# Two-layer graph convolution on one core: who issues the row-by-row tiles, the edges and the broadcasts of the inverse counts

## The chip, the core and the metric

The kernel runs on one core of one Trainium2 chip. The metric is the time of one execution on the device in microseconds (us). PE is TensorE, DVE is VectorE, ACT is ScalarE, POOL is GpSimd and SP is SyncE, which only issues transfers here.

## What is computed

Two layers of an edge-conditioned graph convolution over 6250 nodes with 128 features and 100000 edges with 64 features, edges sorted by destination, then a layer norm of the sum with the input:

```python
def _cgconv(x, src, dst, edge_attr, Wf, bf, Ws, bs, gamma, beta, rmean, rvar):
    z = jnp.concatenate([x[dst], x[src], edge_attr], axis=-1)
    msg = jax.nn.sigmoid(z @ Wf + bf) * jax.nn.softplus(z @ Ws + bs)
    summed = jax.ops.segment_sum(msg, dst, num_segments=n)
    cnt = jax.ops.segment_sum(jnp.ones((dst.shape[0],), x.dtype), dst, num_segments=n)
    out = summed / jnp.maximum(cnt, 1.0)[:, None]
    out = (out - rmean) * jax.lax.rsqrt(rvar + BN_EPS) * gamma + beta
    return out + x
x = _layernorm(x + two_layers(x), axis=-1)
```

## The kernel before

**Tiling.** Edges are padded to 49 groups of 2048. A group has 4 slots (`j`), a slot has 4 tiles of 128 edges, seven groups are a body (`k`), and a layer is 7 bodies: 196 slots, numbered on through the layer in what follows. The first body is written out, the other six are a loop (`Fori`), whose end jumps back five times a layer. Transfers are issued by SP, and gathers by POOL.

**Before the loop.** PE multiplies all node columns with the source half of the weights, ACT copies the result out, and SP stores it as rows of `s_dram` (the source term of z @ W for every node, 256 numbers, 1 KB). The first seven slots of a layer don't wait for that and gather plain node rows.

**A slot.** POOL gathers the source rows of its four tiles into one of 7 places of `pre` (`gather`, L409), by the source numbers in `ends`; it waits until softplus has freed the place seven slots back. DVE overwrites the destination half of the edge columns `lhs` with a transposed one-hot (`hot_transposed`, L791). PE multiplies `lhs`, that is one-hot and edge features, with `rhs` (`product`, L527) into one of two banks `pre_ps`. DVE adds this to the gathered rows in `pre` (`sums`, L815). ACT then has five activations for the slot: two exponentials (L632, L633), two logarithms (L637, L639) and the gate's exponential (L643). DVE makes softplus (L819) and the message (L826), PE sums the messages over the destinations with a one-hot (L801) in a window of 64 nodes (`window_sum`, L548), and DVE adds the window to `sums` (L851). ACT also copies the destination term into `rhs` two slots ahead (L626) and window columns (L649), and reads the windows' bases once a group (`next_bases`, L656).

DVE's order in the step of slot m is fixed: L791 for m, the one-hot L801 for m, L851 for m-4, L815 for m-1, L819 and L826 for m-2. ACT's order is L626, L649, L632, L633, L637, L639, L643.

**SP in the loop (`one`, L353).** For each half group (two slots) SP waits for a product (L362), loads the edge columns of two slots into one of two places of `lhs` (L267, 512 KB), at the first half also the next group's `ends` and bases (L222, L263), and then does a part of the work for a single tile: tile 3 of slot 27 of each body (`SINGLE`) isn't gathered by POOL. SP fetches its block number and its 128 source numbers into `sp_src`, reads 12 of them at a time into registers (L331), and issues one transfer of 1 KB for each row (L335) into `single`; at the end of the body one transfer places them in `pre` (L342).

**Waits.** An instruction carries a wait for a semaphore, and the waits that don't fit are instructions of their own. `done(eng, sems, g, j, lag)` waits for the slot `lag` back.

**Between the layers (`invert_counts`, L235).** In its tail layer 1 writes the counts of edges per node to memory (L241), reads them back spread over 128 partitions (L243), DVE inverts them (L843, L845), SP writes them (L245) and broadcasts the inverses to all partitions in five pieces (L248). SP waits for all of it, and then the layer ends for all engines. Layer 2 begins on DVE with five pairs L760 and L763, which make the nodes of layer 2 out of `sums` and the inverses.

Of the kernel before, what the change touches and what calls it, by code (L numbers as in the profile page):

```python
# [1 line left out]

# [5 lines left out]
ALU = mybir.AluOpType  # L8
# [7 lines left out]
P = 128  # L16
# [27 lines left out]
SINGLE = (BODY - 1, SLOTS - 1, TILES - 1)  # L44
SINGLE_ROWS = 12
# [14 lines left out]
GENERAL_AT = GROUPS + 1  # L60
TABLE_ROWS = GENERAL_AT + GENERAL_GROUPS + 2

# [11 lines left out]
def graph_layer(nc, t, d, layer):  # L74
    first = layer == 1
    with nc.cleanup_on_exit(), ExitStack() as ctx:
# [5 lines left out]
        sp_tab = sb("sp_tab", [1, ROW + 1], I32)  # L82
# [9 lines left out]
        sp_blk = sb("sp_blk", [1, 1], I32)  # L92
        sp_src = sb("sp_src", [1, P], I32)
        single = sb("single", [P, F2], F32)
# [40 lines left out]
        list_in, singles_in, single_in = sem("list_in"), sem("singles_in"), sem("single_in")  # L135
        passed = sem("waits_passed")
        if first:
            dsts_in, ends_of_pairs_in, bn_in = sem("dsts_in"), sem("ends_of_pairs_in"), sem("bn_in")
            iotas, cleared, gen_ready, filled = sem("iotas"), sem("cleared"), sem("gen_ready"), sem("filled")
            table_out = sem("table_out")  # L140
            flagged, plan, fast_ready = sem("flagged"), sem("plan_chain"), sem("fast_ready")
            split, bias_split = sem("bias_parts"), sem("bias_split")
# [10 lines left out]
            fast_rows = sb("fast_rows", [1, GROUPS + 2, ROW], I32)  # L153
# [3 lines left out]
        else:  # L157
            rows_turned, rows_staged, rows_out = sem("rows_turned"), sem("rows_staged"), sem("rows_out")
            scaled = sem("scaled")
# [60 lines left out]
        def _(sp):  # L220
# [4 lines left out]
            if first:  # L225
                load_ends(0, 0)
                sp.dma_start(t["w_node"][:, 0, F2:2 * F2], d["w_node"][0, :, F2:2 * F2]).then_inc(w_src_in, 16)
                for c in range(CHUNKS):
                    sp.dma_start(t["x_t"][:, CUTS[c]:CUTS[c + 1]], d["xT"][:, CUTS[c]:CUTS[c + 1]]
                                 ).then_inc(x_in[c], 16)  # L230
                    if c == 2:
                        sp.dma_start(t["w_node"][:, 0, 0:F2], d["w_node"][0, :, 0:F2]).then_inc(w_in, 16)
                sp.dma_start(t["w_node"][:, 1, :], d["w_node"][1]).then_inc(w_in, 16)

            def invert_counts():  # L235
                cnt_row = t["cnt_dram"].rearrange("(a n) -> a n", a=1)
                cnt_cols = t["cnt_dram"].rearrange("(p c) -> p c", p=P)
                inv_row = t["inv_dram"].rearrange("(a n) -> a n", a=1)
# [14 lines left out]
            def entries(at, n, top):  # L253
                return nc.values_load_multi_w_load_instructions(
                    sp_tab[:, at:at + n], engines=[ENG.SP], min_val=0, max_val=top,
                    skip_runtime_bounds_check_because="every entry of the table is clamped")[1]

            def load_table(row):
                sp.dma_start(sp_tab[:], table[bass.ds(row, ROW + 1)].rearrange("(a c) -> a c", a=1)
                             ).then_inc(sp_tab_in, 16)  # L260
# [8 lines left out]
            def read_plan():  # L269
# [6 lines left out]
                load_table(at)  # L276
# [31 lines left out]
            def load_list(b, half):  # L308
                if half == 0:
                    sp.dma_start(sp_blk[:], table[bass.ds(at + group_no(b, SINGLE[0]) * ROW, 1)].rearrange(  # L310
                        "(a c) -> a c", a=1)).then_inc(list_in, 16)
                    return
                sp.wait_ge(list_in, b * 32 + 16)
                sp.sem_inc(passed, 1)
                blk = sp.value_load(sp_blk[:, 0:1], min_val=0, max_val=GROUPS - 1)
                tile = 2 * (SINGLE[1] * TILES + SINGLE[2])
                sp.dma_start(sp_src[:], d["ends"][bass.ds(blk * P, P), tile:tile + 1].rearrange("p c -> c p")
                             ).then_inc(list_in, 16)

            def load_singles(b, part):  # L320
                if part == 0:
                    sp.wait_ge(list_in, b * 32 + 32)
                    sp.sem_inc(passed, 1)
                    if isinstance(b, int):
                        for r in range(len(s_stage)):
                            sp.wait_ge(s_out[r], stores_of(r))
                    else:
                        sp.wait_ge(single_in, b * 16)
                        sp.sem_inc(passed, 1)
                rows = range(part * SINGLE_ROWS, min((part + 1) * SINGLE_ROWS, P))  # L330
                at_row = nc.values_load_multi_w_load_instructions(  # L331
                    sp_src[:, rows[0]:rows[-1] + 1], engines=[ENG.SP], min_val=0, max_val=NPAD - 1,
                    skip_runtime_bounds_check_because="sources are rows of the table")[1]
                for p, r in zip(rows, at_row):
                    sp.dma_start(single[p:p + 1, :], s_dram[bass.ds(r, 1), :]).then_inc(singles_in, 16)  # L335

            def place_singles(b, g):
                sp.wait_ge(singles_in, b * (16 * P) + 16 * P)
                sp.sem_inc(passed, 1)
                done(sp, s_soft, g, SINGLE[1], RING)  # L340
                sp.sem_inc(passed, 1)
                sp.dma_start(pre[:, slot(*SINGLE[0:2]), SINGLE[2], :], single[:]  # L342
                             ).then_inc(single_in, 16)

            def singles(b, half):
                if half < 2:
                    load_list(b, half)
                elif (half - 2) * SINGLE_ROWS < P:
                    load_singles(b, half - 2)
                if half == 2 * BODY - 1:  # L350
                    place_singles(b, group_no(b, SINGLE[0]))

            def one(b, k):  # L353
                g = group_no(b, k)
                sp.wait_ge(sp_tab_in, g * 16 + 16)
                sp.sem_inc(passed, 1)
                blk, = entries(0, 1, GROUPS - 1)
                blk_next, = entries(1 + GPAIRS, 1, GROUPS - 1)
                load_table(at + (g + 1) * ROW)
                for j in range(0, SLOTS, 2):  # L360
                    done(sp, s_prod, g, j, 3)
                    sp.sem_inc(passed, 1)  # L362
                    if not (isinstance(g, int) and g == 0):
                        load_edges(j, blk * GROUP + j * STEP)
# [7 lines left out]
                    singles(b, 2 * k + j // 2)  # L372
# [5 lines left out]
            sp.wait_ge(sp_tab_in, groups * 16 + 16)  # L378
# [5 lines left out]
        def _(pool):  # L384
            if first:
                nc.gpsimd.memset(fast_rows[:], 0).then_inc(cleared, 1)
                nc.gpsimd.iota(gen_rows[:, :, 0], [[1, GROUPS]], base=0, channel_multiplier=0).then_inc(gen_ready, 1)
                nc.gpsimd.iota(gen_rows[:, :, 1:ROW], [[0, GROUPS], [0, GPAIRS]], base=0, channel_multiplier=WIN
                               ).then_inc(gen_ready, 1)
                pool.wait_ge(cleared, 1)  # L390
                nc.gpsimd.iota(fast_rows[:, 0:GROUPS, 0], [[1, GROUPS]], base=0, channel_multiplier=0
                               ).then_inc(cleared, 1)
# [10 lines left out]
                pool.wait_ge(gen_ready, 2)  # L403
# [10 lines left out]
            if first:  # L414
# [3 lines left out]
                pool.dma_start(table_rows[0:GROUPS + 1, :].rearrange("(a r) c -> a r c", a=1),  # L418
                               fast_rows[:, 0:GROUPS + 1, :]).then_inc(table_out, 16)
                pool.dma_start(table_rows[TABLE_ROWS - 2:TABLE_ROWS, :].rearrange("(a r) c -> a r c", a=1),  # L420
                               fast_rows[:, GROUPS:GROUPS + 2, :]).then_inc(table_out, 16)
# [718 lines left out]
```

## Time and profile before

| | |
|---|---|
| time, median of 3 runs | 2084.61 us (2081.55 to 2085.21) |
| the profiled execution | 2084.45 us, its span 2082.7 us |
| PE, matmuls | 1531.5 us, 74% of the span |
| DVE | 1741.5 us, 84% |
| ACT | 1618.2 us, 78% |
| POOL | 1485.8 us, 71% |
| mean granted clock of TensorE | 0.942 |
| POOL, L409 | 1498 gathers, 1416.8 us |
| DMA engines, mean | 163 GB/s |

Busy times leave out register, branch, semaphore and transfer-issuing instructions, and an engine's share is a mean over prologue, layers and tail. `SPq` and `ACTq` in the rows below are those engines' sequencers, which issue transfers and run register instructions.

### The profile page before, as it was taken

To read this page: it belongs to the slowest core of one execution; us is meant where nothing else is said; L and a number is where in the kernel's file an instruction comes from. 1 tells how busy PE (TensorE), PEld (TensorE's weight loads), DVE (VectorE), ACT (ScalarE), POOL (GpSimd) and SP (SyncE) were. 2 spreads that over 40 slices of the span, in tenths; PEclk is the share of its full clock that TensorE was granted. 3 is DMA by queue.
4 is the path that set the end of the run, shared out by engine and by line. 5 is a ranking of instruction groups with operands and counts; after the bars stand their busy time and mean duration, and the time that the engine had idled before them with its cause. 6 is when DMAs were issued, how large, how long until landed. Compare 5 with 4: busy or idle time off the path is not lost. (4 is left out here: it accounts for less than half of the span.)

```text
span 2082.7 us, 41091 instructions
## 1 busy us (share of the span) xinstructions
PE 1531.5 (74%) x8321; PEld 1258.9 (60%) x8321; DVE 1741.5 (84%) x3576; ACT 1618.2 (78%) x3692; POOL 1485.8 (71%) x1579
## 2 busy tenths in 40 slices
PE   6877777767777777677587777777677777776773
PEld 5766666656566666566476566565556566665662
DVE  3799998979889888798648999798888887988887
ACT  3799887878778777787467888787787787977884
POOL 7577777777777777777257777777777777777770
PEclk8999999999999999999799999999999998999995
DMA  8455555555555555555375555555555555555552
GB/s 282 121 161 171 170 160 159 169 160 160 160 164 163 163 162 162 160 158 162 130 244 160 170 169 169 157 164 167 158 162 160 162 164 159 166 164 158 161 148 62
DMA packets 168890, 339.48 MB, mean 163 GB/s; under 512 B 62702, under 2 KB 93030, under 8 KB 168643
## 3 DMA queue, kind: packets, MB, share of 16 engines
q0 software_dynamic: 73824, 200.29, 32.4%
q1 hardware_dynamic: 93298, 135.27, 21.7%
q10 hardware_dynamic: 1522, 1.72, 0.3%
q14 instruction: 223, 1.83, 0.3%
q8 instruction: 23, 0.38, 0.1%
HBM read 315.49 MB, written 19.81 MB: 161 GB/s over the span
## 5 line engine op out<-in xcount | busy, mean ns | idle before, releaser
L409 POOL DMA_INDIRECT pre<-s_rows,ends x1498 | 1416.8, 946 | 477.9 <-issue 444.9
L527 PE MATMUL pre_ps<-rhs,lhs 128*128 128x256 f32 x3136 | 825.3, 406 | 459.3 <-DVE lhs L791 458.5
L527 PEld LDWEIGHTS pre_ps<-rhs,lhs 128*128 128x128 f32 x3136 | 588.2, 197 | 675.5 <-DVE lhs L791 425.5
L815 DVE TENSOR_TENSOR pre<-pre_ps,pre 128x1024 f32<-128x1024 f32 x378 | 460.6, 1218 | 53.9 <-DMA pre<-s_rows,ends 52.7
L632 ACT ACTIVATE logs<-pre 128x512 f32<-128x512 f32 x392 | 246.9, 630 | 304.5 <-DVE pre L815 268.6
L791 DVE SCALAR_TENSOR_TENSOR lhs<-lhs,base_f,sum_ps 64x256 f32<-64x256 int32 x784 | 374.1, 477 | 107.0 <-issue 52.8
L548 PEld LDWEIGHTS sum_ps<-hot,msg 128*128 128x128 f32 x3136 | 431.4, 200 | 44.7 <-issue 14.0
L548 PE MATMUL sum_ps<-hot,msg 128*128 128x64 f32 x3136 | 411.7, 276 | 19.7 <-DVE sums L851 19.7
L626 ACT COPY rhs<-dst_ps 64x256 f32<-64x256 f32 x792 | 290.0, 366 | 54.0 <-issue 27.3
L826 DVE TENSOR_TENSOR msg<-soft_ps,logs 128x512 f32<-128x512 f32 x392 | 271.1, 691 | 13.3
L819 DVE SCALAR_TENSOR_TENSOR soft_ps<-soft_ps,pre 128x512 f32<-128x512 f32 x392 | 270.4, 690 | 1.1 <-ACT soft_ps L639 1.1
L512 PE MATMUL dst_ps<-w_node,x_cols 128*128 128x256 f32 x792 | 263.1, 415 | 6.2 <-ACT rhs L626 4.2
L637 ACT ACTIVATE logs<-logs 128x512 f32<-128x512 f32 x392 | 246.7, 629 | 12.5
L851 DVE TENSOR_TENSOR sums<-sums,sum_ps 128x64 f32 (+1 forms) x784 | 195.1, 249 | 57.1 <-PE sum_ps L548 4.7
L633 ACT ACTIVATE logs<-pre 128x512 f32<-128x512 f32 x392 | 240.4, 613 | 0.0
L643 ACT ACTIVATE logs<-logs 128x512 f32<-128x512 f32 x392 | 240.2, 613 | 0.0
L639 ACT ACTIVATE soft_ps<-logs 128x512 f32<-128x512 f32 x392 | 228.3, 582 | 0.0
L801 DVE TENSOR_TENSOR hot<-sum_ps,rel 128x256 f32<-128x256 f32 x392 | 166.3, 424 | 12.3
L649 ACT COPY x_cols<-x_t 128x64 f32 x784 | 153.2, 242 | 9.5
L512 PEld LDWEIGHTS dst_ps<-w_node,x_cols 128*128 128x128 f32 x792 | 122.8, 196 | 9.7 <-issue 9.6
L514 PE MATMUL dst_ps<-bias_b,ones_b 128*128 128x256 bf16 x396 | 108.7, 275 | 0.0
L409 POOL DMA_INDIRECT pre<-x_rows,ends x56 | 53.4, 954 | 25.7 <-issue 16.2
(95 smaller groups left out, 575.3 us busy)
## 6 DMA issues: line engine op xcount, KB each, us to landing
lhs<-dge_and_destination_cols SPq DMA_DIRECT2D x196, 512.0 KB
single<-s_rows SPq DMA_DIRECT2D x1792, 1.0 KB
pre<-s_rows,ends POOLq DMA_INDIRECT x1498, 2.8
s_rows<-logs SPq DMA_DIRECT2D x8, 512.0 KB
s_rows<-x_t SPq DMA_DIRECT2D x7, 512.0 KB, 9.4
s_rows<-msg SPq DMA_DIRECT2D x6, 512.0 KB, 10.0
x_rows<-pre SPq DMA_DIRECT2D x12, 256.0 KB
out<-y_out SPq DMA_DIRECT2D x12, 256.0 KB, 2.3
```

What stands on the lines that cost most here:

```text
L409: nc.gpsimd.indirect_dma_start(pre[:, slot(k, j), i, 0:width], None, rows, bass.IndirectOffsetOnAxis(ap=ends[:, k, j * TILES + i, 0:1], ax ...
L512: nc.tensor.matmul(dst_ps[:], x_cols[:, j].rearrange("p q w -> p (q w)"), t["w_node"][:, layer - 1, 0:F2], start=True, stop=False)
L527: ins = nc.tensor.matmul(pre_ps[:, j % 2, i, :], lhs[:, j // 2, edges], rhs[:, j, i // 2, :], start=True, stop=not plain(b, k, j))
L548: ins = nc.tensor.matmul(sum_ps[:, q, 0, 0:WIN], msg[:, j, 2 * q + i, :], hot[:, j, 2 * q + i, :], start=i == 0, stop=i == 1)
L626: ins = nc.scalar.copy(rhs[hot_rows[q], j, q, :], dst_ps[hot_rows[q], :])
L632: nc.scalar.activation(logs[:, j % 2, :, 0:F], pre[:, at, :, 0:F], ACT.Exp, scale=-1.0)
L633: nc.scalar.activation(logs[:, j % 2, :, F:F2], pre[:, at, :, F:F2], ACT.Exp).then_inc(s_expo[j], 1)
L637: nc.scalar.activation(logs[:, j % 2, :, 0:F], logs[:, j % 2, :, 0:F], ACT.Ln, bias=1.0).then_inc(s_log_f[j], 1)
L791: ins = nc.vector.scalar_tensor_tensor(lhs[hot_rows[q], j // 2, at], lhs[hot_rows[q], j // 2, at].bitcast(I32), base_f[hot_rows[q], k, PAI ...
L815: nc.vector.tensor_tensor(rows, pre_ps[:, j % 2], rows, ALU.add).then_inc(s_pre[j], 1)
L819: nc.vector.scalar_tensor_tensor(soft_ps[:, j % 2], soft_ps[:, j % 2], SOFT_TOP, pre[:, at, :, F:F2], ALU.min, ALU.max).then_inc(s_soft[j], 1)
L826: nc.vector.tensor_tensor(msg[:, j], soft_ps[:, j % 2], logs[:, j % 2, :, 0:F], ALU.mult).then_inc(s_msg[j], 1)
```

## The change

1. POOL gathers 109 tiles a body and not 111. Three tiles a body are now loaded row by row. SP loads tile 3 of slots 15 and 26 (`SP_TILES`), which the host leaves with 104 edges each by spreading the padding over them (`SHORT_ROWS`), ACT loads tile 3 of slot 27 with 128 rows (`ACT_TILE`). `SP_PARTS` says which rows SP issues in which half group.
2. ACT reads 12 row numbers into registers in every second slot from slot 2 of a body on (`row_numbers`) and issues six rows a slot: one behind each of L632, L633, L637 and L639, two behind L643 (`load_row`).
3. All loads of edge columns move from SP to ACT, which issues them behind the rows that follow L643 of every odd slot (`load_edges`). The last one of a layer loads columns that nobody reads, and SP waits for it before the layer ends, ahead of `invert_counts`.
4. Block numbers are read once a body, 12 (SP) and 8 (ACT) at a time, and not once a group.
5. SP places ACT's tile at the start of the next body (`place_act`), and its own two in half groups 7 and 13.
6. Layer 1 ends once the inverses are in memory. SP issues the five broadcasts as its first work of layer 2, and DVE waits for each piece (`inv_in`).
7. Small ones: `single` is cleared once a layer (so that the 24 rows nobody loads are finite), semaphores of the prologue are merged, and the table has ten more rows at either end.

```diff
+SP_TILES = ((3, 3), (6, 2))
+ACT_TILE = (6, 3)
+SHORT_ROWS = 104
+SP_PARTS = ((0, 0, 12), (0, 12, 32), (0, 32, 44), (0, 44, 60), (0, 60, 72), (0, 72, 92), (0, 92, 104),
+            (1, 0, 16), (1, 16, 28), (1, 28, 48), (1, 48, 60), (1, 60, 76), (1, 76, 88), (1, 88, 104))
+LIST_AT, PLACE_AT = (BODY + 4, 3), (BODY, 2 * BODY - 1)
+ACT_FROM, ACT_ROWS = 2, 6
+            else:
+                inv_row = t["inv_dram"].rearrange("(a n) -> a n", a=1)
+                for c in range(CHUNKS):
+                    sp.dma_start(t["sums"][:, 1, CUTS[c]:CUTS[c + 1]],
+                                 inv_row[:, CUTS[c]:CUTS[c + 1]].to_broadcast([P, CUTS[c + 1] - CUTS[c]])
+                                 ).then_inc(inv_in[c], 16)
...
                 sp.wait_ge(cnt_moved, 48)
-                for c in range(CHUNKS):
-                    sp.dma_start(t["sums"][:, 1, CUTS[c]:CUTS[c + 1]],
-                                 inv_row[:, CUTS[c]:CUTS[c + 1]].to_broadcast([P, CUTS[c + 1] - CUTS[c]])
-                                 ).then_inc(cnt_moved, 16)
-                sp.wait_ge(cnt_moved, 48 + 16 * CHUNKS)
...
+            def load_rows(i, lo, hi):
+                at_row = nc.values_load_multi_w_load_instructions(
+                    sp_src[:, i, lo:hi], engines=[ENG.SP], min_val=0, max_val=NPAD - 1,
+                    skip_runtime_bounds_check_because="sources are rows of the table")[1]
+                for p, r in zip(range(lo, hi), at_row):
+                    sp.dma_start(single[p:p + 1, i, :], s_dram[bass.ds(r, 1), :]).then_inc(singles_in, 16)
...
                 for j in range(0, SLOTS, 2):
                     done(sp, s_prod, g, j, 3)
                     sp.sem_inc(passed, 1)
-                    if not (isinstance(g, int) and g == 0):
-                        load_edges(j, blk * GROUP + j * STEP)
...
+            place_act(bodies)
+            for j in range(0, SLOTS, 2):
+                sp.wait_ge(edge_in[j // 2], groups * 16 + 16)
             sp.sem_inc(passed, 1)
             if first:
                 invert_counts()
...
-                    gather(s_dram, F2, k, j, TILES - ((k, j) == SINGLE[0:2]))
+                    gather(s_dram, F2, k, j, TILES - ((k, j) in SINGLES))
...
+            def load_edges(g, j, blk):
+                done(act, s_prod, g, j, 0)
+                act.sem_inc(passed, 1)
+                act.dma_start(lhs[:, j // 2, :], d["edge_cols"][:, bass.ds(blk * GROUP + (j - 1) * STEP, 2 * STEP)]
+                              ).then_inc(edge_in[j // 2], 16)
...
+            def load_row(at_rows):
+                for p, r in islice(at_rows, 1):
+                    act.dma_start(single[p:p + 1, len(SP_TILES), :], s_dram[bass.ds(r, 1), :]).then_inc(act_rows_in, 16)
...
                 nc.scalar.activation(logs[:, j % 2, :, 0:F], pre[:, at, :, 0:F], ACT.Exp, scale=-1.0)
+                load_row(at_rows)
                 nc.scalar.activation(logs[:, j % 2, :, F:F2], pre[:, at, :, F:F2], ACT.Exp).then_inc(s_expo[j], 1)
+                load_row(at_rows)
...
                 nc.scalar.activation(logs[:, j % 2, :, 0:F], logs[:, j % 2, :, 0:F], ACT.Exp, scale=-1.0
                                      ).then_inc(s_gate[j], 1)
+                load_row(at_rows)
+                load_row(at_rows)
...
-                    exponents(g, j, slot(k, j))
-                    logarithms(g, j)
-                    gate(g, j)
+                    at_rows = row_numbers(b, SLOTS * k + j, at_rows)
+                    exponents(g, j, slot(k, j), at_rows)
+                    logarithms(g, j, at_rows)
+                    gate(g, j, at_rows)
+                    if j % 2:
+                        load_edges(g, j, of_body[k + 1])
...
                 for c in range(CHUNKS):
                     cols = slice(CUTS[c], CUTS[c + 1])
+                    v.wait_ge(inv_in[c], 16)
                     nc.vector.tensor_tensor(t["sums"][:, 0, cols], t["sums"][:, 0, cols], t["sums"][:, 1, cols],
                                             ALU.mult).then_inc(scaled, 1)
```

## Rows read from the trace of the kernel before

**Rows 1.** One line's instructions (L409), bodies 1 and 2 of layer 1: durations in ns, first and last start in us

```profile
L409 POOL DMA_INDIRECT pre<-s_rows,ends x111: 942/946/955, 171.8 to 309.4; - x111
L409 POOL DMA_INDIRECT pre<-s_rows,ends x111: 942/946/955, 310.6 to 448.2; - x111
```

**Rows 2.** The same view of L632, five stretches of layers 1 and 2

```profile
L632 ACT ACTIVATE logs<-pre x22: 629/630/631, 191.3 to 286.2; 128x512 f32<-128x512 f32 x22
L632 ACT ACTIVATE logs<-pre x23: 629/630/631, 1217.9 to 1314.6; 128x512 f32<-128x512 f32 x23
L632 ACT ACTIVATE logs<-pre x22: 629/630/632, 96.3 to 191.3; 128x512 f32<-128x512 f32 x22
L632 ACT ACTIVATE logs<-pre x168: 624/630/632, 191.3 to 1010.1; 128x512 f32<-128x512 f32 x168
L632 ACT ACTIVATE logs<-pre x168: 624/630/632, 1217.9 to 2032.6; 128x512 f32<-128x512 f32 x168
```

**Rows 3.** Timeline of DVE and ACT at the end of body 1: start, duration, idle before

```profile
317.41 0.97 DVE L791 SCALAR_TENSOR_TENSOR lhs<-lhs,base_f,sum_ps 64x256 f32<-64x256 int32 x2 [4.74 <-issue]
...
324.13 0.98 DVE L791 SCALAR_TENSOR_TENSOR lhs<-lhs,base_f,sum_ps 64x256 f32<-64x256 int32 x2 [2.19 <-PE sum_ps L537]
...
320.64 0.63 ACT L632 ACTIVATE logs<-pre 128x512 f32<-128x512 f32 x1 [5.24 <-DVE pre L815]
...
321.82 0.63 ACT L637 ACTIVATE logs<-logs 128x512 f32<-128x512 f32 x1
...
322.88 0.61 ACT L643 ACTIVATE logs<-logs 128x512 f32<-128x512 f32 x1
326.12 0.74 ACT L626 COPY rhs<-dst_ps 64x256 f32<-64x256 f32 x2 [2.63 <-issue]
```

**Rows 4.** SP's transfers: L335 over the whole run, and a timeline of SP

```profile
L335 SPq DMA_DIRECT2D single<-s_rows x1792: 224/228/290, 60.7 to 2006.5; - x200
...
1221.05 4.84 SPq L335 DMA_DIRECT2D single<-s_rows  x12
1226.79 0.35 SPq L267 DMA_DIRECT2D lhs<-dge_and_destination_cols  x1
```

**Rows 5.** Register work of the sequencers: one stretch of ACT, loads of all bodies

```profile
L199 ACTq FUSED_REGOPS  x2: 37/44/50, 322.5 to 325.2; - x2
...
L656 ACTq TENSOR_LOAD <-base_i x98: 537/547/562, 46.4 to 2016.2; - x98
...
L331 SPq TENSOR_LOAD <-sp_src x154: 719/947/993, 59.6 to 2002.6; - x154
```

**Rows 6.** Timeline of one slot of layer 1, and L851 of layer 2

```profile
223.02 0.63 ACT L632 ACTIVATE logs<-pre 128x512 f32<-128x512 f32 x1 [0.63 <-DVE pre L815]
...
224.20 0.63 ACT L637 ACTIVATE logs<-logs 128x512 f32<-128x512 f32 x1
224.23 0.96 DVE L791 SCALAR_TENSOR_TENSOR lhs<-lhs,base_f,sum_ps 64x256 f32<-64x256 int32 x2
...
225.89 0.74 ACT L626 COPY rhs<-dst_ps 64x256 f32<-64x256 f32 x2
...
227.44 0.63 ACT L632 ACTIVATE logs<-pre 128x512 f32<-128x512 f32 x1 [0.39 <-DVE pre L815]
...
1207.01 0.56 DVE L851 TENSOR_TENSOR sums<-sums,sum_ps 128x64 f32 x2
```

**Rows 7.** Busy time by stretch; the last two columns are DMA share and GB/s

```profile
1230.30:1230.80 0.50, 0.50 (x5) 0.42 (x4) 0.50 (x1) 0.34 (x2) 0.50 (x1) 1.00 0.95 318
1230.80:1231.30 0.50, 0.50 (x5) 0.45 (x3) 0.50 (x2) 0.16 (x1) 0.20 (x2) 1.00 0.19 70
```

**Rows 8.** Timeline between the layers

```profile
1008.88 0.23 SPq L241 DMA_DIRECT2D node_counts<-sums  x1
...
1017.12 0.57 DVE L851 TENSOR_TENSOR sums<-sums,sum_ps 128x64 f32 x2 [2.22 <-PE sum_ps L548]
...
1031.35 0.69 DVE L760 TENSOR_TENSOR sums<-sums 128x512 f32<-128x512 f32 x1
```

More of the change, by code:

```diff
@@ L1 @@
 from contextlib import ExitStack
+from itertools import islice
 import numpy as np
@@ L306, in _ @@
                     store_s(c)
-            def load_list(b, half):
-                if half == 0:
[L310 to L318, printed above, removed]
@@ L323, in load_singles, with singles @@
+            def singles(b, half, blks):
+                if half == 0:
+                    if not isinstance(b, int):
+                        place_act(b)
+                    sp.wait_ge(list_in, b * 32 + 16)
                     sp.sem_inc(passed, 1)
+                    load_list(blks[6], 2, act_list_in)
                     if isinstance(b, int):
@@ L327, in load_singles @@
                     else:
-                        sp.wait_ge(single_in, b * 16)
+                        sp.wait_ge(single_in, b * 32)
                         sp.sem_inc(passed, 1)
[L330 to L351, printed above, removed]
+                if half == PLACE_AT[0]:
+                    sp.wait_ge(list_in, b * 32 + 32)
+                    sp.sem_inc(passed, 1)
+                    place_singles(0, b)
+                load_rows(*SP_PARTS[half])
@@ L377, in _ @@
             sp.wait_ge(base_in[0], bodies * 16 + 16)
-            sp.wait_ge(sp_tab_in, groups * 16 + 16)
+            sp.wait_ge(sp_tab_in, bodies * 16 + 16)
+            sp.wait_ge(list_in, bodies * 32 + 16)
+            sp.sem_inc(passed, 1)
+            place_act(bodies)
+            for j in range(0, SLOTS, 2):
+                sp.wait_ge(edge_in[j // 2], groups * 16 + 16)
             sp.sem_inc(passed, 1)
@@ L689, in _ @@
             if first:
[L690 removed]
+                n = [0]
                 def after(ins):
@@ L1104 @@
     x_t[:, :NODES] = a["x"].T
-    dst = np.full((EPAD + P,), NO_NODE, a["dst"].dtype)
-    dst[:EDGES] = a["dst"]
+    short = np.array([(g * SLOTS + j) * TILES + TILES - 1 for g in range(GROUPS) for k, j in SHORT if g % BODY == k])
+    used = np.ones((EPAD // P, P), bool)
+    used[short, SHORT_ROWS:] = False
+    place = np.flatnonzero(used)[:EDGES]
+    last = np.arange(PAIR - 1, EPAD, PAIR)
+    last[short // (TILES // PAIRS)] -= P - SHORT_ROWS
+    in_order = np.full((EPAD + P,), NO_NODE, a["dst"].dtype)
+    in_order[:EDGES] = a["dst"]
+    dst = np.full((EPAD,), NO_NODE, a["dst"].dtype)
+    dst[place] = a["dst"]
     ends = np.zeros((EPAD, 2), a["src"].dtype)
-    ends[:EDGES, 0] = a["src"]
-    ends[:, 1] = dst[:EPAD]
+    ends[place, 0] = a["src"]
+    ends[:, 1] = dst
     features = np.zeros((FE, EPAD), a["edge_attr_64"].dtype)
-    features[:, :EDGES] = a["edge_attr_64"].T
+    features[:, place] = a["edge_attr_64"].T
     features = features.reshape(FE, EPAD // STEP, PAIRS, PAIR)
-    ends_row = dst[:EPAD].view(features.dtype).reshape(EPAD // STEP, PAIRS, PAIR)
+    ends_row = dst.view(features.dtype).reshape(EPAD // STEP, PAIRS, PAIR)
     edge_cols = np.empty((P, EPAD // STEP, PAIRS, PAIR), features.dtype)
```

177 lines of the change are left out of this document (120 added, 57 removed).

## The prediction

> **What bounds the kernel now.** I read the profile in this order. First the busy shares: DVE 84%, ACT 78%, PE 74%, POOL 71%; none is full, so a share alone says nothing. Then POOL's gathers alone, as POOL's busy time leaves out what lies between them: 111 of them begin at 171.8 us and the next 111 at 310.6 us, so a body of 28 slots takes POOL 138.8 us, 1.2505 us a gather, and the same holds for every later body [rows 1]. A gather counts as busy for 0.946 us, the other 0.30 are its own. Then the pace of the other engines, for which the first exponential of each slot (L632) is a good clock: while gathers are in stock a slot takes 94.9/21 = 4.52 us in layer 1 and 96.7/22 = 4.40 us in layer 2 [rows 2]. At the end of a body the loop jumps back: DVE idles 4.74 us, then 2.19 us on PE, 6.9 us together; ACT's own jump costs it 2.63 us [rows 3]. So a body of the chain of DVE, PE and ACT wants 28 x 4.52 + 6.9 = 133.5 us (130.1 in layer 2), POOL 138.8: POOL sets the time, with 5 to 9 us to spare.
>
> **What the change gives POOL.** The short tiles leave 14 x 24 = 336 rows empty where the padding has 352, so there are still 49 groups. It takes 2 of 111 gathers from each of 14 bodies: 28 x 1.2505 = 35.0 us, a body of 136.3 us. That arrives at the end only if the chain still fits under 136.3.
>
> **SP.** It issues 208 rows a body where it issued 128. Twelve took 4.84 us, from one to the next (4.84 - 0.23)/11 = 0.42 with their registers, the first ones longer; I take 0.41 [rows 4]: 85 us. A register load of 12 row numbers takes 0.947 us, 14 of them (16 to 20 numbers in some) some 17 us [rows 5], ends, bases and lists 9 us: 111 of 136 us, and the edges leave it. The placements fall due 14 us (slot 26) and, because DVE jumps in between, 23 us (slot 27) after SP may begin the last half body; rows 7.8, landing 2, issue 0.5, landing 2.3 are 12.6 us, and with jump and reads 20 us for the other. I cost SP at nothing, with 1.4 to 3 us of cover.
>
> **ACT as an engine.** No row of the trace has ACT issuing a small transfer in the loop. SP's rows bound it: 0.23 us if only the transfer itself costs (228 ns), 0.47 if every one meets another (290 ns and the registers' 0.18) [rows 4]. I take SP's 0.41, since ACT's register instructions are as long as SP's. A slot then costs its sequencer six rows, 2.5 us, and every second slot a load of 12 numbers. The trace shows that the sequencer works beside the engine: the first register instruction after L643 in the program starts at 322.5 us [rows 5], when L637 has ended (321.82 + 0.63 = 322.45) but L643 has not begun (322.88) [rows 3]. So it stops at an instruction's wait and not at its execution. Four rows fit between the activations; the two behind L643 (0.82 us) run beside L643 (0.6 us); an edge issue (0.55) and the load of bases (0.55) don't. A group of four slots then wants about 18.5 us of ACT against 18.1 before. Taken alone this fits, 135.7 us a body with the jump. Its new waits have cover: the block numbers are fetched a group ahead, the list of ACT's tile lands some 12 us before slot 2 of the body asks for it, and if it came late every activation behind it would stand.
>
> **The edges.** This is the step that decides. SP used to issue the edges of slots m+3 and m+4 as soon as the product of slot m had ended. ACT issues them after L643 of slot m. Take L632 of slot m as zero.
> a) The issue. L637 ends at 224.20 + 0.63 - 223.02 = 1.81 us [rows 6]. Rows 3 and 4 of the slot stand behind L637 and L639 and end at 1.20 + 0.82 = 2.02, so L643 is passed at 2.03; rows 5 and 6 end at 2.85; the wait and the registers ahead of the transfer 0.2: it is issued at 3.05 us.
> b) The landing. An edge transfer issued at 1226.79 [rows 4] keeps the DMA engines at 0.95 until 1230.8, and the next slice has 0.19 [rows 7]: 3.5 to 4.0 us; I take 3.8.
> c) What it must reach. DVE builds the transposed one-hot (L791) of slot m+3 when the edges are in. In the trace L791 starts 224.23 - 223.02 = 1.21 us after an L632, and that is slot m+2's; slot m+3's comes one slot later, at 1.21 + 4.52 = 5.7 us, or 6.1 at POOL's new pace of 4.87. The edges come at 3.05 + 3.8 = 6.85.
> d) The way back. From L791 of slot m+3, DVE's fixed order leads over the one-hot and the sums to the sum of slot m+2 (L815) and L632 of slot m+2: 227.44 - 224.23 = 3.21 us [rows 6]; in layer 2 L851 takes 0.56 and not 0.70, so 3.07.
> So two slots can't take less than 3.05 + 3.8 + 3.21 = 10.06 us. Add 0.12 for issues that meet one of SP's: a row took 224 to 290 ns [rows 4], I take 0.03 for each of four. A pair: 10.18 us in layer 1, 10.04 in layer 2, where POOL would allow 9.74.
>
> The trace's answer to whether a transfer can overtake an instruction that waits is the register instruction at 322.5 us: behind L643 it came 0.04 us after what L643 waits for, though ACT had stood for over 5 us before L632 and the whole slot could have been taken in [rows 3, 5]. The Trainium skill (Advanced Engine Details and Errata, Sequencer Loop and Engine Queue Depths) says that engine instructions are pushed into a queue, eight deep on ScalarE, where they wait for their semaphores, and that the sequencer executes control instructions itself. Read so, rows and edges would go out while L632 still waits, the edges would be in time, and the sum would be that of the first rival below. On this point the trace does not agree.
>
> **The sum.** Eleven pairs of a body have rows ahead of the edges, two don't (issue at 1.81 + 0.04 + 0.2 = 2.05, pair 9.06), and one holds the jump: 9.04 + 6.9 + 1.3, the last for what ACT now does between L639 and L626 there (an edge issue and eight block numbers of 0.55 us). Layer 1: 11 x 10.18 + 2 x 9.06 + 17.2 = 147.3 us. Layer 2: 11 x 10.04 + 2 x 8.92 + 17.0 = 145.2.
> Layer 1: slot 7 at 96.3, nine pairs, one of 9.1 and a slot of 4.6 bring slot 28 to 201.6 where it was 191.3: +10.3. From there to slot 195 six bodies less a slot and a jump, 871.0, for 818.8 [rows 2]: +52.2. Layer 2: first body +6 by the same count, then 858.5 for 814.7: +43.8.
>
> **Between the layers.** SP used to wait for the five broadcasts before the layer ended; DVE had ended at 1017.69 and began layer 2's L760 at 1031.35 [rows 8]. Without that wait the layer would end with DVE and some 9 us come back. But SP now waits, before it touches the counts, for the last edges, which nobody uses: ACT issues them 2.05 us after L632 of slot 195 (1010.1), and they land at 1015.9, where SP wrote the counts at 1008.88. The counts go through memory twice, and DVE waits for them in its tail: 7 us later. Gain 2 us, with bounds of -3 and +9. Behind it the stores of x1's rows queue after the broadcasts on SP; if they come late POOL starts layer 2 late, but the chain, not POOL, is what I find last there. The memsets of `single`, the merged semaphores and the longer table cost nothing: DVE waits for inputs or broadcasts there; without that cover 2 x 0.7 us.
>
> 10.3 + 52.2 + 6 + 43.8 - 2 = +110 us on the profiled execution's 2084.45 (span 2082.7; the median shown is 2084.61): **2195 us**.
>
> **Rivals.**
> *The edges are in time.* If the issue comes 0.74 us sooner for each of 150 pairs the loss is gone (110/150), and at 1.0 us POOL sets the time: 2084.45 - 35.0 - 2 = 2047 us. For it: the eight-value load on ACT (547 ns) costs the engine nothing today [rows 5], so a row could be cheaper beside an activation than on SP. Against it: even rows of 0.23 us, the bare issue, gain only 0.54, and the register instruction at 322.5. The queue rule of the Trainium skill (Advanced Engine Details and Errata, Engine Queue Depths) would lead here too, if transfers count among what the sequencer runs ahead with.
> *ACT serialises.* A DMA issue that waits for the activation ahead of it: five activations of 0.61 us, 2.46 of rows, 1.16 of copies (227.44 - 0.39 - 225.89), 0.67 of loads and edges are 7.35 us a slot with rows, 197 us a body, some 2870 us in all. Against it: the load beside L643.
> *Both limits meet.* Lateness of 0.1 to 0.3 us a pair is eaten by POOL's saving: 2080 to 2110.
> *The shared generator.* The Trainium skill (Perfetto Trace Analysis, DMA Instruction, HWDGE) says that sequencers take one descriptor generator in turn, under a lock. By rows, each of four issues that waits 0.06 us (290 less 228) adds 0.24 to a pair instead of 0.12: 2213. It is inside the first case.
>
> **Chances and range.** Edges late: 0.77, with a range of its own from 2114 (rows of 0.23 us) to 2250 (landing 4.0, rows 0.45). In time: 0.13. Meeting: 0.05. Serial: 0.05. The range 2100 to 2285 leaves out the second and the last. 0.2% (4 us) is about what a measurement of this kernel can tell from no change: faster 0.14, same 0.03, slower 0.83.
>
> **What would show it.** In the profile after: DVE idle ahead of L791's successor, put down to the edge transfer, some 150 times and 1 us each; L632 in pairs of 10.1 us; POOL idle on DVE's softplus in every body. Wrong if POOL still has 1.25 us a gather without a wait, or if ACT's sequencer issues rows while L632 waits.

## The result: 2231 us, 7% slower, and the profile after

The changed kernel takes 2231.15 us (median of 4 runs, 2230.43 to 2233.85) and the kernel before 2084.91 (4 runs): the ratio is 1.0707, with a 95% interval from 1.0688 to 1.0725. The forecast was 2195. The profiled execution has a span of 2229.3 us where the one before had 2082.7, so there are 146.6 us to place.

First the page's busy times of the kernel after, as engine, us, share of the span:

```profile
PE 1636.1 (73%) x8321; PEld 1333.9 (60%) x8321; DVE 1752.1 (79%) x3578; ACT 1635.4 (73%) x3692; POOL 1459.6 (65%) x1551
```

DVE has 10.6 us more busy time than before and ACT 17.2, and POOL has 26 less. PE has 104.6 us more for the same 8321 matmuls: its mean granted clock is 0.900 here and was 0.942 before. Whether that made the loss is asked below, under d). All shares have fallen: time went into waiting. The waits of DVE and of POOL in the kernel after say for what; columns are us in total, times, longest:

```profile
DVE lhs L872 <- DMA lhs<-dge_and_destination_cols: 124.9, 116, 2.6
DVE lhs L872 <- PE sum_ps L569: 54.9, 41, 2.4
...
POOL pre L441 <- issue: 481.4, 1389, 2.7
POOL pre L441 <- DVE soft_ps L904: 146.1, 135, 15.8
```

L872 is what L791 was before, the transposed one-hot, and its first wait is for the edges: 116 times, 1.08 us each. Before, it had one such wait:

```profile
L791 DVE SCALAR_TENSOR_TENSOR lhs<-lhs,base_f,sum_ps x784: 461/480/489, 31.0 to 2024.7; 64x256 f32<-64x256 int32 x196
...
  DMA lhs<-dge_and_destination_cols: 1.9, 1
```

POOL now waits 146 us, in 135 places, until DVE's softplus frees a place; before it was 33.3 us in 40. Its gathers of bodies 1 and 3 of layer 1, to compare with [rows 1]:

```profile
L441 POOL DMA_INDIRECT pre<-s_rows,ends x109: 940/946/955, 176.5 to 315.2; - x109
L441 POOL DMA_INDIRECT pre<-s_rows,ends x109: 940/946/948, 465.8 to 615.0; - x109
```

109 gathers at POOL's own pace would be 136.3 us. Body 1 takes 140.8 (the next begins at 317.3), body 3 151.3 (617.1). POOL no longer sets the time. The first exponentials (L704, before L632) do for all stretches what [rows 2] and [rows 8] did:

```profile
L704 ACT ACTIVATE logs<-pre x28: 626/630/631, 55.8 to 199.5; 128x512 f32<-128x512 f32 x28
L704 ACT ACTIVATE logs<-pre x168: 624/630/632, 205.3 to 1089.4; 128x512 f32<-128x512 f32 x168
L704 ACT ACTIVATE logs<-pre x2: 629/630/630, 1089.4 to 1159.7; 128x512 f32<-128x512 f32 x2
L704 ACT ACTIVATE logs<-pre x28: 629/630/631, 1159.7 to 1301.3; 128x512 f32<-128x512 f32 x28
L704 ACT ACTIVATE logs<-pre x168: 623/630/632, 1306.6 to 2179.5; 128x512 f32<-128x512 f32 x168
```

| stretch | before, us | after, us | difference | forecast |
|---|---|---|---|---|
| start to slot 28 | 191.3 | 205.3 | +14.0 | +10.3 |
| slot 28 to slot 195 of layer 1 | 818.8 | 884.1 | +65.3 | +52.2 |
| slot 195 to the first of layer 2 | 69.5 | 70.3 | +0.8 | -2 |
| first body of layer 2 | 138.3 | 146.9 | +8.6 | +6 |
| to the last slot | 814.7 | 872.9 | +58.2 | +43.8 |
| last slot to the end | 50.1 | 49.8 | -0.3 | 0 |

The loss is spread evenly over the bodies, as forecast, and a quarter of it (36 of 146.6 us) was not foreseen. Now one pair of slots of the kernel after in the timeline (start, duration, idle time before); this is the chain of the prediction's a) to d):

```profile
249.94 0.63 ACT L704 ACTIVATE logs<-pre 128x512 f32<-128x512 f32 x1 [0.32 <-DVE pre L900]
250.07 0.23 ACTq L699 DMA_DIRECT2D single<-s_rows  x1
...
252.17 0.61 ACT L719 ACTIVATE logs<-logs 128x512 f32<-128x512 f32 x1
...
252.38 0.61 ACTq L699 DMA_DIRECT2D single<-s_rows  x2
...
253.23 0.37 ACTq L692 DMA_DIRECT2D lhs<-dge_and_destination_cols  x1
...
256.96 0.97 DVE L872 SCALAR_TENSOR_TENSOR lhs<-lhs,base_f,sum_ps 64x256 f32<-64x256 int32 x2 [1.15 <-DMA lhs<-dge_and_destination_cols]
...
260.17 0.63 ACT L704 ACTIVATE logs<-pre 128x512 f32<-128x512 f32 x1 [0.92 <-DVE pre L900]
```

The edges leave 3.29 us behind L704 of the odd slot m (253.23 - 249.94), L872 of slot m+3 starts 3.73 later with the wait put down to them, and L704 of slot m+2 3.21 after that: 10.23 us for two slots. Both rows behind L719 go out at 252.38 and after, while L719 still runs, and the edges stand behind them. The row behind L704 goes out 0.13 us after L704 has started and not in the 0.32 us in which ACT stood for DVE. That is so throughout: ACT stands idle for more than 0.15 us ahead of 253 of the 392 instructions L704, and no transfer leaves its sequencer in any of these stretches.

### The profile page after: what moved, and what is told of

Read it like the earlier page. It is cut to its first block and busy times, and to the rows that moved or that the text cites. A ratio compares the mean times of both kernels' runs of the same rounds, so it can differ in the third digit from the quotient of the medians.

```text
span 2229.3 us, 49874 instructions
## 1 busy us (share of the span) xinstructions
PE 1636.1 (73%) x8321; PEld 1333.9 (60%) x8321; DVE 1752.1 (79%) x3578; ACT 1635.4 (73%) x3692; POOL 1459.6 (65%) x1551
## 5 line engine op out<-in xcount | busy, mean ns | idle before, releaser
L441 POOL DMA_INDIRECT pre<-s_rows,ends x1470 | 1390.5, 946 | 611.1 <-issue 465.0
L559 PE MATMUL pre_ps<-rhs,lhs 128*128 128x256 f32 x3136 | 900.7, 435 | 473.4 <-DVE lhs L872 467.9
L559 PEld LDWEIGHTS pre_ps<-rhs,lhs 128*128 128x128 f32 x3136 | 634.2, 213 | 705.3 <-DVE lhs L872 382.0
L872 DVE SCALAR_TENSOR_TENSOR lhs<-lhs,base_f,sum_ps 64x256 f32<-64x256 int32 x784 | 374.7, 478 | 281.1 <-DMA lhs<-dge_and_destination_cols 124.9
L580 PEld LDWEIGHTS sum_ps<-hot,msg 128*128 128x128 f32 x3136 | 452.1, 208 | 55.2 <-issue 19.3
L900 DVE TENSOR_TENSOR pre<-pre_ps,pre 128x1024 f32<-128x1024 f32 x378 | 460.5, 1218 | 0.2 <-issue 0.2
L580 PE MATMUL sum_ps<-hot,msg 128*128 128x64 f32 x3136 | 425.9, 283 | 24.6 <-DVE sums L936 24.6
L704 ACT ACTIVATE logs<-pre 128x512 f32<-128x512 f32 x392 | 246.7, 629 | 230.7 <-DVE pre L900 198.1
L544 PE MATMUL dst_ps<-w_node,x_cols 128*128 128x256 f32 x792 | 267.8, 421 | 38.1 <-ACT rhs L658 35.2
L719 ACT ACTIVATE logs<-logs 128x512 f32<-128x512 f32 x392 | 240.3, 613 | 0.1
```

The costliest lines, as they stand in the source:

```text
L441: nc.gpsimd.indirect_dma_start(pre[:, slot(k, j), i, 0:width], None, rows, bass.IndirectOffsetOnAxis(ap=ends[:, k, j * TILES + i, 0:1], ax ...
L544: nc.tensor.matmul(dst_ps[:], x_cols[:, j].rearrange("p q w -> p (q w)"), t["w_node"][:, layer - 1, 0:F2], start=True, stop=False)
L559: ins = nc.tensor.matmul(pre_ps[:, j % 2, i, :], lhs[:, j // 2, edges], rhs[:, j, i // 2, :], start=True, stop=not plain(b, k, j))
L580: ins = nc.tensor.matmul(sum_ps[:, q, 0, 0:WIN], msg[:, j, 2 * q + i, :], hot[:, j, 2 * q + i, :], start=i == 0, stop=i == 1)
L704: nc.scalar.activation(logs[:, j % 2, :, 0:F], pre[:, at, :, 0:F], ACT.Exp, scale=-1.0)
L872: ins = nc.vector.scalar_tensor_tensor(lhs[hot_rows[q], j // 2, at], lhs[hot_rows[q], j // 2, at].bitcast(I32), base_f[hot_rows[q], k, PAI ...
```

## The experiments

Means over pairs, here and below, are worked out from the starts of L704, L692 and L872 in the timelines, over the ten pairs of a body (slots 3 to 21) that have rows ahead of the edges, bodies 1 to 6: 60 pairs a layer. In the kernel after they give issue 3.08 and 3.09 us (layers 1 and 2), landing 4.02 and 4.06, way back 3.21 and 3.12, pair 10.32 and 10.27. Landing runs from the issue to the start of L872, so it is longer than the transfer where DVE itself comes late. Over the pairs whose wait is put down to the edges it is 3.99 (44 pairs) and 4.03 (49).

### Edges back on SyncE

```diff
                     done(sp, s_prod, g, j, 3)
                     sp.sem_inc(passed, 1)
+                    if not (isinstance(g, int) and g == 0):
+                        load_edges(j, of_body[k] * GROUP + j * STEP)
...
-                    if j % 2:
-                        load_edges(g, j, of_body[k + 1])
```

The wait for the last, unused edges goes with it.

> The changed kernel with one part undone: SyncE issues the edge columns again, at the start of its half group, before its rows; ScalarE keeps its 128 rows. If late edges are the whole loss, L872 waits for no edge transfer, a body falls from 149 to 136 to 139 us (GpSimd's 136.3, or the loop jump), and the time is 2045 to 2085 us. If ScalarE's rows themselves cost the chain (its activations pushed apart, or the transfers sharing a generator), most of the loss stays: 2150 us or more.

Measured: 2065.5 us (2064.22 to 2065.62), ratio 0.9913 (0.9896 to 0.9929). The edges' place is the loss. ScalarE's rows by themselves are not: they are all still there. POOL's gathers of bodies 1 to 5 of this kernel are at its own pace again:

```profile
L440 POOL DMA_INDIRECT pre<-s_rows,ends x546: 942/946/957, 175.3 to 856.8; - x182
```

545 gathers of 1.2505 us are 681.5 us, and 856.8 - 175.3 is that: 136.3 a body. One thing I had not expected: DVE still waits for edges here, 44 times and 74.3 us in all. SyncE, which now has them beside 208 rows a body with their lists, hardly ever waits for a product any more, so it is probably SyncE that issues them late; the issues themselves were not followed:

```profile
DVE lhs L869 <- DMA lhs<-dge_and_destination_cols: 74.3, 44, 6.2
...
SPq L391 <- PE pre_ps L561: 11.2, 2, 6.4
```

In the kernel after the second of these rows was

```profile
SPq L391 <- PE pre_ps L559: 204.8, 96, 6.0
```

with the edges off SyncE: 96 waits, where e1 has 2. "SyncE at nothing" held only as long as the edges were off it.

### The edges between the two rows, ahead of both, and behind the first exponential

Three kernels move the issue alone and keep every row and every engine's work.

```diff
@@ e2: the edges of an odd slot between the two rows behind L719
                 load_row(at_rows)
+                if edges is not None:
+                    load_edges(g, j, edges)
                 load_row(at_rows)
@@ e3: ahead of both
+                if edges is not None:
+                    load_edges(g, j, edges)
                 load_row(at_rows)
                 load_row(at_rows)
@@ e4: behind L704 of the odd slot
                 nc.scalar.activation(logs[:, j % 2, :, 0:F], pre[:, at, :, 0:F], ACT.Exp, scale=-1.0)
+                if edges is not None:
+                    load_edges(g, j, edges)
                 load_row(at_rows)
```

> ScalarE issues the edges between the two rows behind L719 and not behind both: 0.41 us sooner in the ten pairs of a body that have rows there. If the issue sets the pair: 14 bodies x 10 x 0.41 = 57 us less, 2174 us. If something else does (the rows as such, the landing, the generator): within 10 us of 2231.

> Edges ahead of both rows behind L719: 0.82 us sooner. If the issue sets the pair: 115 us less than 2231, 2116 us, still above GpSimd's bound, because the pairs without rows (9.5 and 9.7 us) and the four slots round the jump (26.9 us) have not changed: 9.5 + 10 x 9.5 + 9.7 + 26.9 = 141 us a body. If GpSimd's bound were met in each pair on its own (9.74), 2150 us. If the rows as such cost: 2200 us or more.

> Edges behind L704 of the odd slot, when the product they wait for has long ended: some 2.7 us sooner (1.7 in pairs without rows). If the issue sets the pair, L872 finds its edges in memory and a body takes 136.3 to 139 us: 2045 to 2085 us, about as with SyncE issuing them. If the placing of an issue ahead of L706 costs ScalarE more than it gives DVE, 2090 us or more, with DVE's softplus waiting for L714.

| | time, us | ratio (95%) | issue | landing | way back | pair |
|---|---|---|---|---|---|---|
| after | 2231.15 | 1.0707 (1.0688 to 1.0725) | 3.08 | 4.02 | 3.21 | 10.32 |
| e2 | 2180.29 | 1.0463 (1.0441 to 1.0485) | 2.66 | 4.11 | 3.22 | 10.00 |
| e3 | 2146.28 | 1.0290 (1.0250 to 1.0329) | 2.27 | 4.14 | 3.33 | 9.74 |
| e4 | 2053.16 | 0.9851 (0.9835 to 0.9868) | | | | |

The last four columns are means of layer 1. The waits for the edges, e2 and then e3:

```profile
DVE lhs L872 <- DMA lhs<-dge_and_destination_cols: 92.1, 110, 2.1
```

```profile
DVE lhs L872 <- DMA lhs<-dge_and_destination_cols: 81.1, 117, 2.7
```

A row ahead of the edges costs 0.42 and 0.39 us of issue, the 0.41 of the prediction, and the time follows: 51 us for the first row where 57 were expected, 34 for the second. 2116 us for e3 was wrong by 30. Its issue came 0.81 us sooner, as expected, and a pair became only 0.58 (layer 1) and 0.64 us (layer 2) shorter: the way back grew by 0.12 and 0.15, and the landing by 0.12 and 0.02. The longer landings are those of DVE and not of the transfer, since in the pairs whose wait is put down to the edges it is still 4.04 and 3.98. What lengthened the way back was not traced. The expectation's other case for e3, 2150 us from POOL's bound met in each pair, is close in number only: DVE's sum L900 never waits for a gather there, and POOL still waits 103 times, 69.8 us, for softplus.

e4 takes the third step. Its edges leave at L704, or before it:

```profile
256.74 0.36 ACTq L692 DMA_DIRECT2D lhs<-dge_and_destination_cols  x1
256.88 0.39 ACT L729 COPY x_cols<-x_t 128x64 f32 x2
257.14 0.95 POOL L441 DMA_INDIRECT pre<-s_rows,ends  x1 [0.30 <-issue]
257.17 0.62 ACT L704 ACTIVATE logs<-pre 128x512 f32<-128x512 f32 x1
```

L692 stands behind L704 in the program and goes out 0.43 us before L704 starts. What L704 waits for had come, and L704 only queued behind ScalarE's copies. So the sequencer stops at a wait and not at an execution, now seen with a transfer. The Trainium skill (Advanced Engine Details and Errata, Sequencer Loop) has engine instructions wait in a queue for semaphores while others are read; these rows agree with a queue of instructions whose waits are met, and no row shows a transfer that passes a wait still open. POOL's gathers of bodies 1 to 5 in e4, and L872's waits:

```profile
L441 POOL DMA_INDIRECT pre<-s_rows,ends x546: 942/946/956, 169.6 to 851.0; - x182
```

```profile
L872 DVE SCALAR_TENSOR_TENSOR lhs<-lhs,base_f,sum_ps x784: 461/480/490, 32.2 to 1996.2; 64x256 f32<-64x256 int32 x196
...
  DMA lhs<-dge_and_destination_cols: 2.3, 1
```

One wait for edges is left of 116, and a body takes POOL's 136.3 us. e4, which has all parts of the change, is 31 us faster than the kernel before; part 1 alone had been put at 35. Moving one call turned 7% slower into 1.5% faster than before.

### ScalarE without its rows

POOL gathers tile 3 of slot 27 again (110 gathers a body, 137.6 us); the edges stay at their place behind L719. SyncE no longer fetches the list of ScalarE's tile and no longer places it.

```diff
-                    gather(s_dram, F2, k, j, TILES - ((k, j) in SINGLES))
+                    gather(s_dram, F2, k, j, TILES - ((k, j) in SP_TILES))
...
-                if step < ACT_FROM or (step - ACT_FROM) % 2:
+                if True:
                     return left
```

It ran twice. Beside the first run the kernel before took 2926 us and not 2084; so it did beside e7, e6, e8, e11 and e12 below. What that was is asked at the end.

> The changed kernel without ScalarE's tile: GpSimd gathers tile 3 of slot 27 again (110 gathers a body, 137.6 us), SyncE keeps its two tiles, ScalarE only issues the edges, at its place behind L719. Every pair then has the issue of the pairs without rows, 2.05 us behind L704. If only issue plus landing plus way back count: pairs of 9.5 us in layer 1 and 9.25 in layer 2 and 26.9 us for the four slots round the jump, 141 and 138 us a body, 2100 us (2090 to 2115): moving the edges alone loses. If the rows on ScalarE's queue also lengthen the landing (4.05 us on average now), the landing falls to 3.8 or less and the time to 2070 to 2085.

e5: 3148.77 us (3080.77 to 3181.95), against 2926; the ratio is 1.0800 (1.0735 to 1.0865), but its four runs lie from 5% to 9% above the kernel before, so its size is uncertain.

> The kernel of e5 again, since e5's chip ran the kernel before at 2926 us. As there: if only issue, landing and way back count, pairs of 9.5 us (layer 1) and 9.25 (layer 2), 2100 us (2090 to 2115), slower than the 2084 before although ScalarE issues not one row. If the rows lengthened the landing, 2070 to 2085.

e9, with 2084.06 for the kernel before: 2086.68 us (2079.12 to 2089.95, 10 runs), ratio 1.0009 (1.0000 to 1.0018). That is no change that can be told, between the two expectations. The means decide: issue 2.08 and 2.05, landing 4.08 and 4.07, way back 3.21 and 3.12, pair 9.37 and 9.24. The landing is what it was with the rows (4.10 and 4.01 in the pairs that wait for the edges), so the rows did not lengthen it. 2100 was too high, since I had taken 9.5 for layer 1 from the two pairs without rows that the kernel after has. Ten pairs of 9.37, two more near 9.1 and 27.2 round the jump are 139 us a body in layer 1, longer than POOL's 137.6 and than the 138.8 of before; layer 2 has 137, and there POOL decides: its 552 gathers of bodies 1 to 5 start 1.2506 us apart. L868 still waits 102 times for edges, for 46.0 us. Two tiles on SyncE gain nothing while the edges are issued that late.

### SyncE's wait for the last edges

```diff
+            if first:
+                invert_counts()
             for j in range(0, SLOTS, 2):
                 sp.wait_ge(edge_in[j // 2], groups * 16 + 16)
             sp.sem_inc(passed, 1)
-            if first:
-                invert_counts()
```

> The changed kernel with SyncE's wait for the last, unused edges behind invert_counts and not ahead of it. The counts leave 6.8 us sooner. If DVE's tail waits for them, 4 to 6 us less than 2231: 2226 us. If the layer's end is set by something else, within 2 us.

e7 (this edit on the kernel after): 3296.93 us, ratio 1.1180 (1.1110 to 1.1251), against 2926; what 5 us do can't be read from it.

> e4 (edges behind the first exponential of the odd slot, 2053 us) with SyncE's wait for the last, unused edges behind invert_counts. In e4 the counts left SyncE late as well, and DVE idled 3.6 us for them in its tail. The tail goes through without a wait, and the last L844 starts 29.5 us behind the layer's last L704 and not 34: 4 to 5 us less, 2048 to 2050. If the layer change is set elsewhere, 2053 as e4.

e10 (this edit on e4): 2050.97 us (2047.62 to 2053.06), ratio 0.9845 (0.9832 to 0.9858). Against e4's 0.9851 the medians can't tell 2 us. The profiles can tell the stretch from slot 195 to layer 2's first slot, e4 first, then e10:

```profile
L704 ACT ACTIVATE logs<-pre x2: 629/630/630, 995.0 to 1065.7; 128x512 f32<-128x512 f32 x2
```

```profile
L704 ACT ACTIVATE logs<-pre x2: 630/630/630, 992.7 to 1058.1; 128x512 f32<-128x512 f32 x2
```

70.7 us against 65.4, 5.3 less where 4 to 5 were expected. DVE's first instruction on the counts, in e4 and in e10:

```profile
1002.50 0.19 DVE L928 TENSOR_SCALAR cnt<-cnt 128x50 f32<-128x50 f32 x1 [3.62 <-DMA cnt<-node_counts]
```

```profile
996.61 0.19 DVE L928 TENSOR_SCALAR cnt<-cnt 128x50 f32<-128x50 f32 x1
```

The wait in DVE's tail is gone. e10 is the best kernel of the study by its median.

### The layer change alone, and two transfers for two slots

e8 and e12 are one kernel: the one before with part 6 of the change (the five broadcasts of the diff in front, first on SyncE in layer 2, with DVE's wait for each). e6 and e11 are the changed kernel with each edge load as two transfers of 256 KB:

```diff
-                act.dma_start(lhs[:, j // 2, :], d["edge_cols"][:, bass.ds(blk * GROUP + (j - 1) * STEP, 2 * STEP)]
-                              ).then_inc(edge_in[j // 2], 16)
+                for e in (j - 1, j):
+                    act.dma_start(lhs[:, j // 2, e % 2 * STEP:(e % 2 + 1) * STEP],
+                                  d["edge_cols"][:, bass.ds(blk * GROUP + e * STEP, STEP)]).then_inc(edge_in[e], 16)
```

> The kernel before with part 6 alone: the layer ends with the inverses in memory, the five broadcasts are SyncE's first work of layer 2, DVE waits for each piece. SyncE and DVE end within 2 us of each other, so the wait of 13.3 us for the broadcasts turns into the first broadcast's landing, and the later pieces arrive one by one: 5 us less than before, 2080 us. If the pieces or the start of the layer cost as much as the wait did, 2084 to 2086.

> The kernel of e8 again, for the same reason. In e8's trace the last L765 of the layer change started 29.4 us behind the layer's last L633; in the kernel before it is 34.2. That is 4.7 us less, and as much at the end: 2080 us (2078 to 2082). If the gain is eaten behind the layer change (GpSimd's stock, SyncE's stores later), 2083 to 2086.

> Each edge load as two transfers of 256 KB, one a slot, with a semaphore each, at the same place behind both rows (three prologue semaphores are one here). If the landing is mostly the moving of 512 KB, the half that slot m+3 needs is in 0.7 to 0.8 us sooner and the time goes by e3's measure to 2130 to 2150. If the landing is fixed cost and queueing, the gain is under 0.3 us a pair, 2190 us or more.

> The kernel of e6 again, since e6's chip ran the kernel before at 2926 us. The second transfer adds 0.5 us to ScalarE's sequencer a pair, and slot m+3 waits for 256 KB only. If the landing (4.05 us on average for 512 KB) is mostly the moving of the bytes, 0.7 to 0.8 us less a pair and 2130 to 2150 us; if it is fixed cost and queueing, 2190 us or more.

All four ran beside a kernel before of 2926 us. e8: ratio 1.0023 (0.9991 to 1.0054), e12: 0.9994 (0.9958 to 1.0031). 5 us are 0.17% there, a ratio of 0.9983: that is inside e12's interval and just outside e8's, so a gain of that size is neither shown nor ruled out. e6: 1.1202 (1.1148 to 1.1256), e11: 1.1280 (1.1228 to 1.1332), no better than e7's 1.1180 with whole transfers. But the edges were hardly what DVE waited for there. The one-hot's waits in e6:

```profile
L873 DVE SCALAR_TENSOR_TENSOR lhs<-lhs,base_f,sum_ps x784: 461/481/491, 36.0 to 3275.8; 64x256 f32<-64x256 int32 x196
...
  remote: 946.4, 128
...
  DMA lhs<-dge_and_destination_cols: 23.4, 17
```

"remote" stands for a wait whose end the profile puts down to none of its instructions and transfers. The waits in e8, which loads edges as the kernel before does:

```profile
L793 DVE SCALAR_TENSOR_TENSOR lhs<-lhs,base_f,sum_ps x784: 461/480/490, 38.4 to 2883.9; 64x256 f32<-64x256 int32 x196
its engine sat idle before it (us, times) until:
  remote: 665.4, 133
```

L793 takes 480 ns as in the 2084 us runs, and ahead of it DVE stands 665 us for "remote", 5.0 us at a time; ScalarE has 686.7 us of the same ahead of its copies. The profile of the kernel before at 2084 us has no such row, and no profile of it at 2926 was kept. So whether the split shortens a landing where the landing counts stays open, and so does part 6 by itself in the time. What the profile of e8 gives of it is a distance between two rows: DVE's last L765 (1493.90) starts 29.4 us after slot 195's L633 (1464.5), where the kernel before has 34.2; in e12 it is 30.0.

## Why the prediction was right, and what it had mis-sized

The sign, the mechanism and its place were right, and 2231 lies in the main case's own range; the likeliest value was 36 us too low, most of it by the size of one term, the landing b).

- **POOL's bound.** 136.3 us a body is shown by e1 and e4, to the microsecond. It could not arrive in the changed kernel, as forecast.
- **SyncE at nothing.** Right for the changed kernel: none of DVE's waits is put down to SyncE's tiles, and SyncE stands 204.8 us for products. e1 shows how little is left when the edges are added.
- **The sequencer stops at a wait.** Right: the row behind L704 leaves 0.13 us after L704 starts, and e4's edges overtake an activation that only queues. The rival "the edges are in time" needed rows that cost ScalarE much less than 0.41 us, or transfers that pass an open wait; neither came.
- **ACT serialises.** Ruled out: its price was 197 us a body, and the rows leave while activations run.
- **a) The issue.** 3.05 and the 0.12 for meetings were forecast, 3.08 measured; a row is 0.39 to 0.42, forecast 0.41. The 3.08 is a mean of two values: 2.99 to 3.04 us in most pairs, and 3.21 to 3.34 in two or three of the ten places of a body (the pair shown above, 3.29, is one). Where those 0.3 us come from was not found. The rival of the shared generator, 0.24 us a pair, would have made the mean 3.29.
- **b) The landing.** The term that was mis-sized: 3.8 forecast from one transfer, 4.02 and 4.06 measured, from 3.61 to 5.11. The 3.8 was the end of the DMA engines' busy stretch behind one issue; DVE starts on the edges later than that, 3.99 and 4.03 us after the issue on average where it waits for them. It counts in each pair, and is not the rows' doing (e9).
- **d) The way back.** 3.21 and 3.07 forecast, 3.21 and 3.12 measured. A product lies inside it, and TensorE's mean granted clock was 0.900 where it had been 0.942. The way back of layer 1 did not grow (in most slots of the kernel before it is 3.20 to 3.21, in layer 2 3.07), so the clock did not make the loss. In e4, with the same work, the clock is 0.941 again.
- **The pairs without rows.** 9.06 and 8.92 forecast; 9.48 and 9.74 in layer 1, 9.07 and 9.40 in layer 2, from the landing again. The sum counted eleven pairs that rows delay; there are ten, because the last two rows of a body leave behind the first two activations of its slot 23, whose edges leave 2.04 us behind L704 as in a pair without rows. The four slots round the jump took 26.9 us, where my sum had 27.4, the eleventh pair and the jump's. A body of layer 1: 9.5 + 103.2 + 9.7 + 26.9 = 149.3 us, forecast 147.3. Twelve bodies by about 2.3 us are 28 of the 36 us, the first body of each layer 6, the layer change 3.
- **The break-even.** "The loss is gone" at 0.74 us a pair was wrong: e3 has 0.8 and is still 2.9% slower, because a pair gains only 0.58 to 0.64 us of it, and the loss to make good was 146 us and not 110. e9, with 1.0 us and no rows, breaks even; e4 wins.
- **Between the layers.** -2 us forecast, +0.8 measured. The counts did leave late: 5.6 us behind slot 195's exponential (1094.97 - 1089.4) and not 1.2 ahead of it [rows 8], 6.8 us where 7 were forecast. The first product with the inverses came as forecast too, 19.4 us behind instead of 21.2. What I had left out is that the broadcasts then arrive piece by piece:

```profile
1108.78 0.69 DVE L841 TENSOR_TENSOR sums<-sums 128x512 f32<-128x512 f32 x1 [2.93 <-DMA sums<-node_inverses]
...
1111.74 1.22 DVE L841 TENSOR_TENSOR sums<-sums 128x1024 f32<-128x1024 f32 x1 [1.48 <-DMA sums<-node_inverses]
...
1115.29 1.76 DVE L841 TENSOR_TENSOR sums<-sums 128x1536 f32<-128x1536 f32 x1 [1.01 <-DMA sums<-node_inverses]
```

DVE waits for three of the five, and 2.5 us are lost behind the first. With the wait for the last edges out of the way (e10) the stretch is 65.4 us where the kernel before has 69.5: 4.1 us gained, so the bound of 9 us was too high.

## What to carry to other kernels

A transfer that is issued from a computing engine's stream starts no earlier than the waits ahead of it in that stream: place it right behind the wait that it really needs, and put filler transfers behind it. Before a load is moved to another queue, add up the loop that it closes (issue, landing, way back to the next issue); once that loop is longer than the other bound, each transfer ahead of it is paid for each time round (here 51 and 34 us for two rows of 0.4 us, in 140 rounds). A load whose result nobody reads still delays whoever is made to wait for it.

## What the runs showed of the hardware beyond this

- A 512 KB load into `lhs` took 3.6 to 5.1 us from issue to the instruction that it released, where the wait is put down to it, on average 3.96 to 4.10 in each layer of the kernel after, e2, e3 and e9, with or without 128 small transfers a body on the same queue.
- A transfer leaves ScalarE's sequencer while the engine still executes what stands ahead of it, 0.43 us before an activation that is ahead in the program (e4). It left ahead of none of the 253 instructions L704 for which the engine stood waiting (kernel after).
- The kernel before took 2926 us beside e5 to e8 and beside e11 and e12, and 2084 in all other runs. In the profiles of the runs beside 2926 us L793 and its like take 480 ns as ever, TensorE's mean granted clock is 0.76 to 0.81, and DVE and ScalarE have "remote" stalls of 4.5 to 7.4 us on average. There the change cost 12% (e7, with its small edit) and the edges on ScalarE without rows 5% to 9% (e5), against 7% and 0.1%. e5 to e8 ran under the same chip number as e9 and e10, so it is not shown that the difference is one of chips. Whether ScalarE's stalls hold the edges back there was only thought of; no run tells.
